# A two-layer decoder on one core: the order of all pieces on every engine fitted anew, and three waits written out

## The reference

```python
x = x + L0_attn(ln(x))            # causal, 16 heads of 16; ternary weights, 8-bit activations
x = x + L0_xattn(w, u, ln(x), ctx)  # a WKV recurrence over time, k = ln(x), v = ctx
x = x + L0_ffn(ln(x))             # sigmoid(x1) * x2, ternary weights, 704 hidden
x = x + L1_attn(ln(x))            # 32 heads of 8, 8 key heads, rotary, not causal
x = x + L1_xattn(ln(x), ctx)      # 32 heads of 8; keys of ctx and of x, windows 64 and 32, alibi
x = x + L1_ffn(ln(x))             # low-rank experts: softmax router, top 2 of 6, plus a dense base
```

```python
no = max(o, u + k); y = (exp(o - no) * p + exp(u + k - no) * v) / (exp(o - no) * q + exp(u + k - no))
```

## Time and profile before

| | |
|---|---|
| runs | 688.61, 689.04, 686.31 us; median 688.61 |
| span of the profiled execution | 691.1 us |
| granted TensorE clock, mean | 0.949 of full speed |
| busy: PE, DVE, ACT, POOL | 613.2, 543.6, 481.4, 392.3 us |
| moved by DMA | 55.11 MB, mean 80 GB/s |

### The profile page before, as it was taken

How to read it: one execution, slowest core, us unless ns; L and a number is a source line. 1 busy time by engine, 2 the same in 40 slices (tenths; PEclk the granted TensorE clock), 3 DMA queues, 4 the chain that set the end, 5 groups by cost and what they waited for, 6 DMA issues and landing times.

```text
span 691.1 us, 20216 instructions
## 1 busy us (share of the span) xinstructions
PE 613.2 (89%) x7368; PEld 372.6 (54%) x7368; DVE 543.6 (79%) x1357; ACT 481.4 (70%) x1185; POOL 392.3 (57%) x745
## 2 busy tenths in 40 slices
PE   6699999856788789999999988789999999999984
PEld 6466666534566568544444344345555556555542
DVE  5889999899899996889998867567777777777521
ACT  4599998996878646577787773467676667666650
POOL 5343786897899958856665312334545544545321
PEclk9799999998899989999999999899999999999995
DMA  8899645111110002444545524353343444433000
GB/s 296 205 220 170 93 94 107 57 58 39 39 39 32 24 11 54 64 78 89 79 79 86 95 58 81 60 89 68 76 82 73 68 80 88 79 76 59 20 9 15
DMA packets 163603, 55.11 MB, mean 80 GB/s; under 512 B 148976, under 2 KB 161456, under 8 KB 163376
## 3 DMA queue, kind: packets, MB, share of 16 engines
q1 hardware_dynamic: 161456, 53.68, 38.1%
q0 software_dynamic: 2048, 0.14, 0.2%
HBM read 16.82 MB, written 5.24 MB: 32 GB/s over the span
## 4 chain that ended last, share of the span: by engine, by line
PE 57%; DVE 18%; issue 7%; POOL 6%; DMA 6%; ACT 4%; SPq 1%; DVEq 0%; ACTq 0%; POOLq 0%
PE bank L1333 4%; PE bank L1266 4%; PE bank L1002 3%; PE bank L1280 3%; PE bank L1678 3%; DMA l1x_qT<-l1x_neg_maxT 3%; DVE mix_num_den L1542 2%; PE bank L1355 2%; PE bank L1305 2%; DMA l1a_kT<-k_stack 2%; PE bank L1287 2%; PE bank L1863 2%; PE bank L976 2%; PE bank L1689 2%; PE bank L1022 2%
## 5 line engine op out<-in xcount | busy, mean ns | idle before, releaser
L1181 DVE TENSOR_REDUCE l1x_neg_max<-bank 128x2 f16<-128x448 f32 (+1 forms) x192 | 116.0, 640 | 46.3 <-PE bank L1287 46.1
L1235 ACT ACTIVATE l1x_probs<-bank 128x512 f32<-128x512 f32 x192 | 104.2, 596 | 57.4 <-PE bank L1309 33.0
L889 DVE TENSOR_REDUCE l1a_neg_max<-bank 128x4 f16<-128x512 f32 x128 | 82.2, 685 | 12.9 <-PE bank L976 11.9
L936 ACT ACTIVATE l1a_probs<-bank 128x512 f32<-128x512 f32 x128 | 69.5, 595 | 21.3 <-PE bank L990 21.3
L1137 POOL DMA_DIRECT2D l1x_qT<-l1x_neg_maxT x64 | 37.5, 592 | 51.7 <-ACT l1x_neg_maxT L1231 51.7
L1678 PE MATMUL bank<-mix_xT_parts,w_ternary 128*128 128x256 f16 x384 | 53.1, 287 | 7.7 <-DVE mix_hidden L1560 7.5
L1678 PEld LDWEIGHTS bank<-mix_xT_parts,w_ternary 128*128 128x128 f16 x384 | 38.5, 103 | 19.8 <-DVE mix_hidden L1560 11.2
L1754 POOL TENSOR_TENSOR moe_logits<-moe_low_rank_logits,router_bias 128x6 f32<-128x6 f32 x16 | 3.3, 206 | 77.4 <-ACT moe_low_rank_logits L1831 77.4
L573 DVE TENSOR_REDUCE l_neg_max<-bank 128x4 f16<-128x512 f32 x64 | 41.5, 674 | 5.7 <-PE bank L698 5.0
L1492 POOL TENSOR_TENSOR mix_hidden_parts<-mix_hidden,mix_hidden_parts 128x256 f16<-128x256 f32 x48 | 38.0, 799 | 8.5 <-ACT mix_hidden_parts L1623 8.1
L642 ACT ACTIVATE l_probs<-bank 128x512 f32<-128x512 f32 x64 | 35.2, 608 | 3.5 <-PE bank L721 1.8
(11 more groups left out here) (271 smaller groups left out, 1814.5 us busy)
## 6 DMA issues: line engine op xcount, KB each, us to landing
ctx_projected<-mix_ctx_projected SPq DMA_DIRECT2D x16, 192.0 KB, 2.0
l1x_ctx_projected<-ctx_projected SPq DMA_DIRECT2D x16, 160.0 KB, 2.4
mix_ctx_in<-ctx_in SPq DMA_DIRECT2D x16, 128.0 KB, 2.1
out_dram<-moe_out SPq DMA_DIRECT2D x16, 128.0 KB, 2.1
x_residual<-x_in SPq DMA_DIRECT2D x1, 1536.0 KB, 10.0
w_f<-w_in SPq DMA_DIRECT2D x2, 704.0 KB, 10.3
...
```

The lines of the kernel that those rows point to most:

```text
L889: dve.tensor_reduce(mm[:, 16 * j + 4 * s:16 * j + 4 * s + 4], b_s[c % 3][:].rearrange("p (r k) -> p r k", k=P), AX.X, ALU.max, negate=True ...
L936: act.activation(prob[:, c, :], b_st[c % 2][:], ACT.Exp).then_inc(s_exp, 1)
L1181: dve.tensor_reduce(mm[:, first:first + count], scores, AX.X, ALU.max, negate=True).then_inc(s_max, 1)
L1235: act.activation(prob[:, c, :], b_st[c % 2][:], ACT.Exp).then_inc(s_exp, 1)
```

## The change

All numbers of `PHASES`, `PACE` and `STEPS` are replaced, and three waits are added on POOL. The pieces and their instructions are the same. One line of each table, and the waits:

```diff
 PHASES = {
     ("l0", "sp"): phases("""
-        G@5.030"""),
+        G@11.448"""),
...
 PACE = {
-    "l0": (-91.729, 19.87, (4.716, 6.971, 8.492, 11.987), 11.788),
+    "l0": (-92.744, 64.448, (7.743, 0.989, 11.287, 13.438), 10.087),
...
-    ("l0", "sp"): (-102.007,),
+    ("l0", "sp"): (212.133,),
...
             if piece == "F1c":
                 pool.wait_ge(s_var, b + 1)
+                wait(pool, s_xn, b - 1)
                 pool.tensor_tensor(rstd[:, bp, :], ve[:, bp, :], net.mhalf[:], ALU.pow).then_inc(s_rstd, 1)
...
             if piece == "F1c":
                 pool.wait_ge(s_f1, b * 3 + 3)
+                wait(pool, s_xn, b - 1)
                 pool.tensor_tensor(rstd[:, bp, :], ve[:, bp, :], net.mhalf[:], ALU.pow).then_inc(s_rstd, 1)
...
             if piece == "LNc":
                 pool.wait_ge(s_lnc, b * 3 + 3)
+                wait(pool, s_xn, b - 1)
                 pool.tensor_tensor(rstd[:, bp, :], ve[:, bp, :], net.mhalf[:], ALU.pow).then_inc(s_rstd, 1)
```

More of the change, by code:

```diff
@@ L160 @@
     ("moe", "pe"): phases("""
[L161 removed]
+        TR@4.989 DOWN@5.104 LORA@5.466 UP@5.815"""),
 }
 PACE = {
[L164 to L168 removed]
+    "l0": (-92.744, 64.448, (7.743, 0.989, 11.287, 13.438), 10.087),
@@ new lines @@
+    ("l0", "pool"): (-159.994,),
+    ("l0", "sp"): (212.133,),
+    ("mix", "act"): (25.496,),
+    ("mix", "dve"): (24.593,),
+    ("mix", "pe"): (12.570,),
+    ("mix", "pool"): (9.553,),
+    ("mix", "sp"): (214.213,),
+    ("l1a", "act"): (141.314,),
+    ("l1a", "dve"): (127.648,),
+    ("l1a", "pe"): (10.265,),
+    ("l1a", "pool"): (102.416,),
+    ("l1a", "sp"): (266.865,),
+    ("l1x", "act"): (323.735,),
+    ("l1x", "dve"): (229.554,),
+    ("l1x", "pe"): (261.795,),
+    ("l1x", "pool"): (267.278,),
@@ L202 @@
+    ("l1x", "sp"): (393.302,),
+    ("moe", "act"): (396.737,),
+    ("moe", "dve"): (392.763,),
+    ("moe", "pe"): (237.284,),
+    ("moe", "pool"): (374.977,),
+    ("moe", "sp"): (327.567,),
+    ("windows", "pool"): (13.635, -73.426, -237.360, -82.249, -174.567, -102.165, -348.656, -241.676, 22.657,),
 }
```

121 lines of the change are left out of this document (49 added, 72 removed).

## The result

| | us | runs |
|---|---|---|
| before | 688.6 median (686.31 to 689.04) | 4 |
| changed | 700.15 median (698.08 to 701.25) | 4 |
| ratio | 1.0163, 95% interval 1.0126 to 1.020 | |

The change makes the kernel slower by 11.5 us between the medians (11.2 by the ratio, 8.7 to 13.8 by its interval). Forecast were 697.8 us and +9.2.

What follows compares the result with a forecast made beforehand. From 60 us on TensorE and VectorE limit in turn, with hardly an idle place. 8 + 0 - 1.4 + 1 - 1.4 + 3 = +9.2 us takes the median of 688.61 to 697.8 us; range 684 to 705.

Steps and rivals of the forecast that it cites:

- Rival B: Start, on SP: batch 0's transposes pass the late loads; around 684 us, faster than before; chance 0.20.
- C: Rival: the start's delay is real, but the mixer's idle time closes; +3.2 us, 691.8 us; chance 0.12.
- signs: Expected in the trace: transposes landed at 36 to 38 us, L703 first at 41 to 43, L1292 14.6 to 15.2 apart.
- Late loads, +12: Start, SP's queue q1: batch 0's transposes land behind 5,709 KB of loads, at some 37.3 us, 12 later; ends +2 and +14.
- Setup order on DVE, 2.1 late and hidden: Setup: sums over attention weights move behind statistics of batches 1 to 3; ternary weights 2.1 us later, hidden under the 12.
- First attention, 4 of the 12 back: Third w_f sum out of the loop (1.7), 16 fewer shape changes (1.6), slow periods (0.7) return 4 us, leaving +8.
- Mixer, 0 ± 6: Mixer: new order of W10, W8 and W4 on DVE, and SP's context loads; taken as 0, kept ±6 us.
- Second attention, -1.4: Second attention, DVE: L873 moves out from between L893 and L898, for about 8 batches; -1.4 us.
- Passage, +1: Passage to the third attention: PE has fewer pieces between batch 0's maxima and their use; +1 us.
- Third attention, -1.4 for the shapes: Third attention with the last stage, PE: 14 fewer changes of tile shape, at 0.10 us each; -1.4 us.
- Third attention, +3 for maxima and store: Third attention: longer waits for the maxima's DMA and for transposes behind the moe_out store; +3 us (0 to +12).
- The three waits, 0: POOL: waits for the normalised x of two batches back, done a period before, hold nothing; 0.

Runs made afterwards that it cites:

- e2: The kernel before, with all 17 late loads issued on SP ahead of batch 0's transposes: 701.62 us, ratio 1.0217.
- e1: The changed kernel, with the 17 late loads back between the transposes of batches 0 to 8: 689.68 us, ratio 1.0048 to before.
- the first group: Late-load runs: changed kernel with loads spread (689.68 us), before with loads first (701.62), changed kernel with loads between batch 0's and batch 1's transposes (699.38).
- e14: e11 with DVE's two sums over the attention weights again ahead of the statistics of batches 1 to 3: 687.35 us, ratio 0.9999 to before.
- e9: The changed kernel without PE's 16 idle matmuls behind batch 0's first scores: 704.34 us, ratio 1.0226 to before.
- e10: The kernel before, with DVE's row statistics (L873) behind the first reduction of the scores in the second attention: 686.88 us, ratio 0.9972.
- e8: The changed kernel with SP's store of moe_out again behind the transposes of the third attention: 695.62 us, ratio 1.0111 to before.
- e11: The changed kernel with late loads spread over batches 0 to 8 and the moe_out store behind the transposes: 689.04 us, ratio 1.0014 to before.
- e4: The kernel before, with only the change's three waits on POOL added: 686.85 us, ratio 0.9989.
- e6: The changed kernel with setup, first attention, mixer and window preparation as before: 691.52 us, ratio 1.0058 to before.

## Why the prediction was right

The sign, the size (+11.5 for +9.2) and the main mechanism were right: batch 0's transposes wait for all late loads in q1. e2 shows it alone (+14.9), e1 its undoing. Rival B is out by all three runs of the first group, and C too: the mixer took nothing up. That the sum was close is partly luck, because terms missed both ways: the start and the first attention lose 6.0 us more than forecast (14.0 for 8), and the stages from the second attention to the end give 5.9 back in the spans, where the forecast had them lose 1.2. Nor did the forecast name anything for the seams of the mixer or for the end behind the last L1292, which is 1.5 us shorter (40.1 us for 41.6).

Of its signs, the issue ahead of 27 us (23.93), the period of L1292 (14.72), the 8.0 us of L981 (8.1 over nine steady periods), the waits for the maxima and the unchanged mixer came. Missed were the landing (38.5 us for 36 to 38) and L703, at 46.0 us for 41 to 43.

- *Late loads, +12.* Measured 13.1: there at 38.54 us, forecast 37.3. Right; 375 GB/s was the fitting row. The last load landed at 36.45 us, forecast 36.4, and the transposes 2.1 us behind it, where the forecast took about 1.
- *Setup order on DVE, 2.1 late and hidden.* Right. DVE's first step on the ternary weights (L311) starts 1.3 us later (13.82 for 12.55), its part of q of batch 0 (L565) 2.8 later (21.25 for 18.41). With the loads away it shows as 2.95 us in e1 and is gone in e14.
- *First attention, 4 of the 12 back.* Wrong, the largest miss: at its end the delay is 14.0, forecast 8. What was forecast to come back inside it does: from the first L703 to batch 14's the delay goes from 15.7 to 11.9. Of that 1.65 is in the first period (6.28 us for 7.93; but other kernels with before's tables have 6.3 there too, so it isn't shown to be the third sum over w_f), and 2.1 in batch 1 to batch 14 (82.3 us for 84.4, a spacing of 6.13 for 6.34 where nothing waits; forecast 6.25). Two losses were at nothing in the sum. First, F5 of batch 2, moved behind batch 0's scores, takes 16 idle matmuls with it, 3.76 us at the low clock: 7.5 us from the first scores to L703 instead of 4.9 (to 30.34 us). Second, the last period, into the mixer, is 2.1 us longer. Taking the matmuls away doesn't pay either (e9).
- *Mixer, 0 ± 6.* Right: 144.7 and 144.8 us from the last L703 to the first L981, with 2.4 us lost in front and won behind.
- *Second attention, -1.4.* -2.1 in the profiles (123.3 for 125.4), -1.9 in e10's medians, -1.0 in e10's nine steady periods: right.
- *Passage, +1.* Wrong: -0.9 (20.8 for 21.7 us).
- *Third attention, -1.4 for the shapes.* Wrong: the price of 0.10 us from two pairs of rows is a difference between neighbours, and the steady period, with one change of shape fewer, didn't move.
- *Third attention, +3 for maxima and store.* Right as mechanisms: waits for the maxima +2.4, and e8 and e11 have 2 to 4 us for the store by the medians. It isn't seen in the stage's length (219.3 for 220.7), as its first four periods got shorter (57.5 for 59.5 us). In them PE's waits at L1280 for DVE's maxima (1.5 us in three periods before) are gone, and those of the first ST for ACT's exponentials are 0.4 us for 1.5; which move did that wasn't taken apart.
- *The three waits, 0.* Right (e4).
- *Rival B* has 0.9 us for the slow periods of the first attention, where the term itself had 0.7; its time moves by 0.2 us.

Put together from the medians: of the 1.63%, 1.15 go with the late loads (e1), 0.34 with the store (e11) and 0.15 with the sums (e14), and nothing is left; each of these is uncertain by about 0.4, so only the first is clear of the noise by itself. With these three orders of before put back, the refit is neither better nor worse than what it replaces (0.9999). The version that beats both is the smallest: before with L873 moved (0.9972, 0.9953 to 0.9992).

**Still open**: which orders shorten the third's first periods, what makes e6's median slower than before, and the other 3.6 us of e9.
